# Where three small pieces of work stand in the order of an attention kernel: a reciprocal, two gate activations and a projection

## The chip, the cores and the metric

The kernel runs on one core of a Trainium2 chip. Its time is the device time of one execution in microseconds. Before the change three executions took 1186.85, 1190.78 and 1191.3 us, the median being 1190.78 us. The profiled execution is a fourth one, and took 1187.66 us.

## The reference

Four sequences of 1024 tokens with 128 channels pass through one block: causal attention with 16 heads of 64 and a bias by distance, a residual and a layer norm, then an RWKV channel mix, a residual and a second layer norm.

```python
q, k, v = einsum('bsx,xMnd->Mbnsd', x, qkv)
a = softmax(einsum('bnsd,bntd->bnst', q, k) * 64**-0.5 + bias)      # bias: cumsum by distance, -30000 above the diagonal
x = layernorm(x + einsum('bnsd,ndx->bsx', einsum('bnst,bntd->bnsd', a, v), out_w))
x_prev = x shifted by one token
r = sigmoid((mu_r * x + (1 - mu_r) * x_prev) @ W_r.T)
k = square(relu((mu_k * x + (1 - mu_k) * x_prev) @ W_k.T))
x = layernorm(x + r * (k @ W_v.T))
```

## The kernel before

Two heads make a pair; 4 sequences times 8 pairs are 32 steps (`PAIR_STEPS`). Every engine has its own program, written out by hand as a loop over the steps and, in each step, over 16 slots (`NROWS`). A slot stands for one score row: one head and one tile of 128 queries, 128 to 1024 keys wide. Slots 0 to 3 are head 0, tiles 0 to 3; 4 to 7 head 1, tiles 0 to 3; 8 to 11 head 0, tiles 4 to 7; 12 to 15 head 1, tiles 4 to 7. No planner moves anything: an engine does its instructions in the order of its own loop, and semaphores hold it until what it needs is there.

A row goes through the engines like this. TensorE (PE) computes its scores four slots ahead (line 954). VectorE (DVE) adds the bias from PSUM and takes the row minimum in one instruction (line 643; the scores are negated, so the minimum is the maximum). ScalarE (ACT) takes the exponential with its sum (line 486), also four slots ahead. In the row's own slot PE transposes its blocks of 128x128 (line 968) into one of two PSUM banks, `ps_t0` and `ps_t1`, which alternate: bank use k may start once use k-2 has been copied out. A row of up to 4 blocks is one bank use, a longer row two. `EVACUATOR` says who copies use k out: DVE (line 667) or ACT (line 504). Uses 8 and 9 belong to slot 8, 10 and 11 to slot 9, 12 and 13 to slot 10, 14 and 15 to slot 11, 16 and 17 to slot 12, 18 and 19 to slot 13, 20 and 21 to slot 14, 22 and 23 to slot 15. Uses 8, 10, 11, 12, 14, 16 and 20 are DVE's, uses 9, 13, 15, 17, 18, 19, 21, 22 and 23 are ACT's. In slot 14 the inverses of the sums (DVE, line 653, issued in slot 13) are transposed as well (line 973).

Between these rows stands other work. The next step's q, k and v are projected in six chunks at `PROJ_SLOTS`, all into the one bank `ps_m`: four chunks of two matmuls of 512 columns (line 929), and two chunks of four blocks for v, in slots 10 and 14 (line 934). ACT copies a v chunk out (line 476) at the beginning of the same slot. The probabilities are multiplied with v in slots 2 and 5 for the upper half of the step before, and in slot 11 for the lower half (line 992).

From step 9 on (`TILE_LAG`), each step also takes one tile of 128 tokens of an earlier sequence through the rest of the block (`tile_step`); step 31 and the code behind the loop do what is left. 23 of the 32 steps have such a tile, and 22 of these (9 to 30) project for a next step too. Slot 0: the output projection (PE line 1006), which needs `mix_tile`, a 512 KB load that SyncE issues at line 353 behind the eight transfers of the k stacks. Slots 1, 2 and 4: first layer norm and token shift. Slot 9: receptance and key projections (PE lines 1011 and 1012), the exponential of the gate and the relu of the key on ACT (lines 521 and 522, semaphore `s_sig`), then 1 + exp and the square on DVE. Slot 11: the gate's reciprocal on DVE (line 713). Slot 12: the v projection (PE line 1016), product with the gate, residual and statistics on DVE. Slot 15: second layer norm (ACT lines 514 and 517, DVE line 724). These tile matmuls also use `ps_m`: a projection chunk or tile matmul starts only when ACT or DVE has read the one before out of it (`wait_chunk`, `wait_tile`). So the v chunk in slot 10 waits for `s_sig`, that is for ACT's relu.

Within a slot the orders that the change touches are these. ACT: copy of a projection chunk, the tile's activations, copies of its bank uses, exponential of the row four slots ahead. DVE: bias and minimum of the row four slots ahead, inversion of sums, `lo` part of a projection chunk, copies of its bank uses, multiplication of a finished mix, the tile's step; in slot 8 alone the copies come first. PE: scores of the row four slots ahead, projection chunk, tile matmul, mix, transposes of the own row.

Of the kernel before, what the change touches and what calls it, by code (L numbers as in the profile page):

```python
# [13 lines left out]
PAIR_STEPS = BATCH * PAIRS  # L14
# [26 lines left out]
def score_at(r):  # L41


    if r < NROWS // 2:
        return BANK * (r % 4)
    width = P * (ROWS[r][1] + 1)
    return SEQ * (r % 2) + ((SEQ - width) // 2 if width - BANK < SHORTEST else 0)
# [22 lines left out]

EVACUATED = [evacuated(engine, NBANKS) for engine in range(2)]

PROJ_SLOTS = (2, 3, 5, 7, 10, 14)
NPROJ = len(PROJ_SLOTS)


OUT_PROJ, LN1_RSTD, LN1 = 0, 1, 2
# [3 lines left out]
RK_PROJ, GATE = 9, 11  # L81
# [11 lines left out]
def build(nc, x, qkv, out_w, rpe, w_r, w_k, w_v, mu_r, mu_k, out):  # L93
# [14 lines left out]
    with ExitStack() as ctx:  # L108
# [6 lines left out]
        def sem(name):  # L115
            return ctx.enter_context(nc.semaphore(name))
# [86 lines left out]
        s_v = sem("v_ready")  # L203
# [58 lines left out]
        def rows_ahead(n, more, slot):  # L262

            if slot + LEAD < NROWS:
                return [(n, slot + LEAD)]
            return [(n + 1, slot + LEAD - NROWS)] if more else []
# [176 lines left out]
        def _(act):  # L443
# [15 lines left out]
            def project(m, c):  # L459

                if c == 0 and m > 0:
                    if m == 1:
                        act.wait_ge(s_first, 96)
                    for h in range(2):
                        act.wait_ge(s_stack[h], 96 * m)
                act.wait_ge(s_proj, NPROJ * m + c + 1)
                if c < 4:
                    which, at = chunk_of(m, c)
                    dst, scale = ((q_hi, SCALE), (k_hi, 1.0))[which]
                    half = slice(512 * at, 512 * at + 512)  # L470
                    nc.scalar.activation(dst[:, half], proj_bank(m, c), ACT.Copy, scale=scale).then_inc(s_hi, 1)  # L471
                else:
                    half = slice(4 * (c - 4), 4 * (c - 4) + 4)
                    if c == 4 and m >= 2:
                        act.wait_ge(s_pv, 2 * m)
                    nc.scalar.activation(v_pair[m % 2][:, half, :],  # L476
                                         proj_bank(m, c).rearrange("p (t d) -> p t d", d=P), ACT.Copy).then_inc(s_v, 1)

            def exps(n, r):

                width = P * (ROWS[r][1] + 1)
                act.wait_ge(s_biased, NROWS * n + r + 3)
                if n > 0 and r % (2 * GROUP) == 0:
                    act.wait_ge(s_inv, 2 * n - 1 + r // (2 * GROUP))
                row = prob[:, r % PSLOTS, 0:width]
                nc.scalar.activation(row, row, ACT.Exp, bias=low[:, r:r + 1], scale=-1.0,  # L486
                                     accum_out=total[:, r:r + 1]).then_inc(s_exp, 1)

            def evacuate(n, k, tile_too):
                r, b0, nb = BANKS[k]  # L490
                h, i = ROWS[r]
                g = i // GROUP
                act.wait_ge(s_pv, 2 * n + g + 1)
                if n == 0 and r == 3 * GROUP:
                    act.wait_ge(s_xt_dram, 16 * (BATCH - 1))
                act.wait_ge(s_tr, NBANKS * (n + 1) + k + 1)
                if k == X1_BANK and tile_too:
                    at = 1 + (n - TILE_LAG) % TILES * P
                    nc.scalar.activation(x1_t[:, at:at + P], ps_t[k % 2][:, P:2 * P], ACT.Copy).then_inc(s_x1t, 1)
                if k == INV_BANK[1]:  # L500
                    if n > 0:
                        act.wait_ge(s_inv_d[1], 16 * n)
                    nc.scalar.activation(inv_t[1][:, :], ps_t[k % 2][0:2 * GROUP, 3 * P:], ACT.Copy).then_inc(s_inv_t[1], 1)
                nc.scalar.activation(pt[h][g][:, b0:b0 + nb, P * (i % GROUP):P * (i % GROUP) + P],  # L504
                                     ps_t[k % 2][:, 0:nb * P].rearrange("p (b s) -> p b s", s=P),
                                     ACT.Copy).then_inc(s_ev[1], 1)
# [33 lines left out]
            def step(n, prev, tile_too, more):  # L540
                for slot in range(NROWS):
                    if more and slot in PROJ_SLOTS:
                        project(n + 1, PROJ_SLOTS.index(slot))
                    if tile_too:
                        tile_step(n, slot)
                    for k in range(NBANKS):
                        if BANKS[k][0] == slot and EVACUATOR[k] == "1":
                            evacuate(n, k, tile_too)
                    for row in rows_ahead(n, more, slot):
                        exps(*row)  # L550

            drive(step)

            def ln_rstd(which, w):
# [48 lines left out]
        def _(dve):  # L603
# [29 lines left out]
            def bias(n, r):  # L633

                h, i = ROWS[r]
                width = P * (i + 1)
                if i % GROUP == 0:
                    dve.wait_ge(s_table[n % 2][h], 16 * (n // 2) + 16)

                before = (r - PSLOTS) % NROWS  # L640
                dve.wait_ge(s_tr, NBANKS * (n if before > r else n + 1) + sum(b[0] <= before for b in BANKS))
                dve.wait_ge(s_score, NROWS * n + r + 1)
                nc.vector.tensor_tensor_reduce(prob[:, r % PSLOTS, 0:width],  # L643
                                               ps_rows[:, score_at(r):score_at(r) + width],
                                               table[n % 2][:, h, 0:width][:, ::-1], 1.0, 3.0e38, ALU.add, ALU.min,
                                               low[:, r:r + 1]).then_inc(s_biased, 1)
# [96 lines left out]
            def step(n, prev, tile_too, more):  # L743
                for slot in range(NROWS):
                    if slot == LATE_SLOT:
                        empty_banks(n, slot)
                    for row in rows_ahead(n, more, slot):
                        bias(*row)
                    if slot in INV_READY:
                        invert(n, INV_READY.index(slot))  # L750
                    if more and slot in PROJ_SLOTS[:4]:
                        project(n + 1, PROJ_SLOTS.index(slot))
                    if slot != LATE_SLOT:
                        empty_banks(n, slot)
                    if prev and slot == MIX_FAR[1] + 1:
                        store_mix(n - 1, 1)
                    if slot == MIX_NEAR + 1:
                        store_mix(n, 0)
                    if tile_too:
                        tile_step(n, slot)  # L760

            drive(step)
# [103 lines left out]
        def _(pe):  # L866
# [28 lines left out]
            def wait_chunk(m, c):  # L895

                if 0 <= c < 4:
                    pe.wait_ge(s_lo, 4 * m + c + 1)
                else:
                    pe.wait_ge(s_v, 2 * m + (c - 3 if c > 0 else 0))  # L900
# [10 lines left out]
            def project(m, c, tile_too):  # L911
# [13 lines left out]
                if tile_too:  # L925
                    wait_tile(m - 1 - TILE_LAG, sum(at < PROJ_SLOTS[c] for at in TILE_MATMULS))
                if c < 4:
# [69 lines left out]
            def tile_step(n, slot, more=False):  # L997
                e = n - TILE_LAG
                if more and slot in TILE_MATMULS:
                    wait_chunk(n + 1, sum(at <= slot for at in PROJ_SLOTS) - 1)  # L1000
                if slot in TILE_MATMULS:
                    wait_tile(e, TILE_MATMULS.index(slot))
                if slot == OUT_PROJ:
                    pe.wait_ge(s_mixt, 16 * e + 16)
                    for p in range(PAIRS):
                        ins = nc.tensor.matmul(ps_m[:, 0:C], mix_tile[:, p, :], wo[:, p, :],  # L1006
                                               start=(p == 0), stop=(p == PAIRS - 1))
                    ins.then_inc(s_e1, 1)
                if slot == RK_PROJ:
                    pe.wait_ge(s_chain, CH * (e + 1) + 6)  # L1010
                    nc.tensor.matmul(ps_m[:, 0:P], xr_t[:, :], w_t[:, 0, :], start=True, stop=True)
                    nc.tensor.matmul(ps_m[:, P:2 * P], w_t[:, 1, :], xk_t[:, :], start=True, stop=True)\
                        .then_inc(s_e6, 1)
                if slot == V_PROJ:
                    pe.wait_ge(s_chain, CH * (e + 1) + 7)
                    nc.tensor.matmul(ps_m[:, 0:C], k_act[:, :], w_t[:, 2, :], start=True, stop=True).then_inc(s_e8, 1)
# [126 lines left out]
```

## Time and profile before

| | |
|---|---|
| median of three executions | 1190.78 us (1186.85 to 1191.3) |
| profiled execution, its own time | 1187.66 us |
| its span | 1185.9 us |
| granted TensorE clock, mean | 0.992 |
| PE busy | 1115.7 us (94%) |
| DVE busy | 811.5 us (68%) |
| ACT busy | 727.4 us (61%) |
| PE's longest wait in total | 23.1 us in 42 waits, for DVE's copies of `ps_t` |

The profile is one execution. The span is what the records cover; 1.76 us of the execution's own time lie around it. From one step's v chunk to the next step's it is 35.40 us in steps with a tile, and 33.24 us in steps without. Busy time of PE counts matmuls with modelled, overlapping ends, so the start of one group to the start of the next tells more than the durations.

### The profile page before, as it was taken

To read this page: it belongs to the slowest core of one execution; us is meant where nothing else is said; L and a number is where in the kernel's file an instruction comes from. 1 tells how busy PE (TensorE), PEld (TensorE's weight loads), DVE (VectorE), ACT (ScalarE), POOL (GpSimd) and SP (SyncE) were. 2 spreads that over 40 slices of the span, in tenths; PEclk is the share of its full clock that TensorE was granted. 3 is DMA by queue.
4 is the path that set the end of the run, shared out by engine and by line. 5 is a ranking of instruction groups with operands and counts; after the bars stand their busy time and mean duration, and the time that the engine had idled before them with its cause. 6 is when DMAs were issued, how large, how long until landed. Compare 5 with 4: busy or idle time off the path is not lost.

```text
span 1185.9 us, 21563 instructions
## 1 busy us (share of the span) xinstructions
PE 1115.7 (94%) x6973; PEld 783.3 (66%) x6973; DVE 811.5 (68%) x2121; ACT 727.4 (61%) x1857; POOL 6.4 (1%) x15
## 2 busy tenths in 40 slices
PE   5999999989999999999999999999999999999994
PEld 3666666666666667666667666676666667767673
DVE  2666666666667677767677767677767677777756
ACT  3666666666666666666566656566656666656632
POOL 1000000000000000000000000000000000000000
PEclk9999999999999999999999999999999999999997
DMA  8865556565655666656657655657665657665610
GB/s 213 215 150 140 136 137 150 136 177 145 154 150 142 158 153 173 160 143 161 157 150 180 159 145 141 151 150 202 155 149 139 150 153 180 155 154 136 223 55 20
DMA packets 113005, 180.71 MB, mean 152 GB/s; under 512 B 13152, under 2 KB 69360, under 8 KB 112896
## 3 DMA queue, kind: packets, MB, share of 16 engines
q1 hardware_dynamic: 110736, 178.42, 59.5%
q8 instruction: 58, 0.95, 0.3%
q10 hardware_dynamic: 2160, 0.92, 0.3%
q14 instruction: 51, 0.42, 0.1%
HBM read 58.41 MB, written 20.22 MB: 66 GB/s over the span
## 4 chain that ended last, share of the span: by engine, by line
PE 82%; DVE 8%; ACT 5%; issue 4%; DMA 1%; DVEq 0%; SPq 0%; POOL 0%; ACTq 0%
PE ps_o L992 22%; PE ps_t L968 21%; PE ps_rows L954 18%; PE ps_m L929 9%; PE ps_m L934 5%; PE ps_m L1006 4%; DVE pt L667 3%; DVE prob L643 3%; ACT prob L486 3%; PE ps_rows L1062 1%; DMA prob<-in_L_attn_x 1%; ACT pt L504 1%; PE ps_t L973 1%; DVE mix_sb L674 1%; ACT xk_t L522 1%
## 5 line engine op out<-in xcount | busy, mean ns | idle before, releaser
L486 ACT ACTIVATE prob<-prob,low 128x128 f32<-128x128 f32 (+7 forms) x512 | 394.6, 772 | 129.4 <-DVE low L643 125.1
L643 DVE CUSTOM_DVE_ANT_0 prob<-ps_rows,table 128x128 f32<-128x128 f32 (+7 forms) x512 | 378.8, 748 | 56.2 <-PE ps_rows L954 55.4
L954 PE MATMUL ps_rows<-stacks 128*128 128x512 f32 (+3 forms) x1536 | 401.9, 372 | 6.3 <-issue 4.4
L968 PE MATMUL ps_t<-ident,prob 128*128 128x128 f32 x2304 | 347.2, 277 | 30.7 <-DVE pt L667 23.1
L968 PEld LDWEIGHTS ps_t<-ident,prob 128*128 128x128 f32 x2304 | 261.0, 140 | 134.7 <-issue 96.2
L667 DVE COPY pt<-ps_t 128x512 f32<-128x512 f32 (+3 forms) x352 | 200.4, 577 | 178.8 <-PE ps_t L968 176.9
L992 PE MATMUL ps_o<-pt,v_pair 128*64 128x512 f32 (+3 forms) x1536 | 268.6, 492 | 0.0
L954 PEld LDWEIGHTS ps_rows<-stacks 128*128 128x128 f32 x1536 | 246.0, 190 | 27.1 <-issue 4.6
L504 ACT ACTIVATE pt<-ps_t 128x512 f32<-128x512 f32 (+3 forms) x416 | 187.2, 466 | 114.6 <-PE ps_t L968 114.3
L992 PEld LDWEIGHTS ps_o<-pt,v_pair 128*64 128x64 f32 x1536 | 101.8, 136 | 181.7 <-issue 172.3
L929 PE MATMUL ps_m<-x_cur,w_cur 128*128 128x512 f32 x250 | 130.8, 605 | 2.5 <-issue 1.6
L471 ACT ACTIVATE q_hi<-ps_m 128x512 fp32r<-128x512 f32 x63 | 37.4, 593 | 122.1 <-PE ps_m L929 121.8
L486 ACT ACTIVATION_READ_ACCUMULATOR prob<-prob,low 128x1 f32 x512 | 97.8, 191 | 0.0
L629 DVE SCALAR_TENSOR_TENSOR q_lo<-ps_m,q_hi 128x512 fp32r<-128x512 f32 x63 | 43.6, 692 | 50.8 <-ACT q_hi L471 50.8
L934 PE MATMUL ps_m<-w_cur,x_cur 128*128 128x128 f32 x504 | 68.0, 278 | 6.4 <-ACT xk_t L522 6.4
L934 PEld LDWEIGHTS ps_m<-w_cur,x_cur 128*128 128x128 f32 x504 | 63.6, 191 | 13.0 <-issue 12.9
L929 PEld LDWEIGHTS ps_m<-x_cur,w_cur 128*128 128x128 f32 x250 | 43.4, 191 | 14.5 <-issue 8.0
L1006 PE MATMUL ps_m<-wo,mix_tile 128*128 128x128 f32 x384 | 47.0, 275 | 0.1
L629 DVE SCALAR_TENSOR_TENSOR k_lo<-ps_m,k_hi 128x512 fp32r<-128x512 f32 x62 | 42.6, 687 | 4.8 <-ACT k_hi L471 4.7
L1006 PEld LDWEIGHTS ps_m<-wo,mix_tile 128*128 128x128 f32 x384 | 44.9, 192 | 0.5 <-issue 0.4
L476 ACT ACTIVATE v_pair<-ps_m 128x512 f32<-128x512 f32 x63 | 37.3, 592 | 12.7 <-PE ps_m L934 11.2
L674 DVE TENSOR_TENSOR mix_sb<-ps_o,inv_all 128x512 f32<-128x512 f32 x64 | 43.6, 681 | 2.0 <-PE ps_o L992 2.0
(114 smaller groups left out, 475.2 us busy)
## 6 DMA issues: line engine op xcount, KB each, us to landing
stacks<-k_hi SPq DMA_DIRECT2D x126, 256.0 KB, 4.5
stacks<-k_lo SPq DMA_DIRECT2D x126, 256.0 KB, 4.9
inv_all<-inverse_sums SPq DMA_DIRECT2D x128, 128.0 KB, 3.3
stacks<-q_hi SPq DMA_DIRECT2D x63, 256.0 KB, 3.8
stacks<-q_lo SPq DMA_DIRECT2D x63, 256.0 KB, 4.3
mix_transposed<-mix_sb SPq DMA_DIRECT2D x62, 256.0 KB, 2.3
table<-bias_by_distance SPq DMA_DIRECT2D x64, 192.0 KB, 3.6
mix_tile<-mix_transposed SPq DMA_DIRECT2D x24, 512.0 KB, 5.3
```

Source lines behind the costliest of these rows:

```text
L486: nc.scalar.activation(row, row, ACT.Exp, bias=low[:, r:r + 1], scale=-1.0, accum_out=total[:, r:r + 1]).then_inc(s_exp, 1)
L504: nc.scalar.activation(pt[h][g][:, b0:b0 + nb, P * (i % GROUP):P * (i % GROUP) + P], ps_t[k % 2][:, 0:nb * P].rearrange("p (b s) -> p b s" ...
L629: nc.vector.scalar_tensor_tensor(out=lo[:, half], in0=proj_bank(m, c), scalar=scale, in1=hi[:, half].bitcast(F32), op0=ALU.mult, op1=ALU.s ...
L643: nc.vector.tensor_tensor_reduce(prob[:, r % PSLOTS, 0:width], ps_rows[:, score_at(r):score_at(r) + width], table[n % 2][:, h, 0:width][:, ...
L667: nc.vector.tensor_copy(pt[h][g][:, b0:b0 + nb, P * (i % GROUP):P * (i % GROUP) + P], ps_t[k % 2][:, 0:nb * P].rearrange("p (b s) -> p b s ...
L674: nc.vector.tensor_tensor(mix_sb[g][:, :], ps_o[:, :], inv_all[g][:, :], ALU.mult).then_inc(s_o, 1)
L929: ins = nc.tensor.matmul(proj_bank(m, c), w_cur[m % 2][:, which, :], x_cur[:, 512 * at:512 * at + 512], start=True, stop=True)
L934: ins = nc.tensor.matmul(proj_bank(m, c)[:, P * t:P * t + P], x_cur[:, at:at + P], w_cur[m % 2][:, 2, :], start=True, stop=True)
L954: ins = nc.tensor.matmul(ps_rows[:, at + c0:at + c1], q_st(h, n)[:, P * i:P * i + P], k_st(h, n, low_part)[:, c0:c1], start=(low_part == 0 ...
L968: ins = nc.tensor.transpose(ps_t[k % 2][:, P * b:P * b + P], prob[:, r % PSLOTS, at:at + P], ident[:, :])
L992: ins = nc.tensor.matmul(ps_o[D * h:D * h + D, c0:], v_pair[n % 2][:, j, D * h:D * h + D], pt[h][g][:, j, c0:], start=(j == 0), stop=(j == ...
L1006: ins = nc.tensor.matmul(ps_m[:, 0:C], mix_tile[:, p, :], wo[:, p, :], start=(p == 0), stop=(p == PAIRS - 1))
```

## The change

Three groups of instructions change place; none is added or removed, but for one semaphore wait on PE.

1. The second v chunk goes from slot 14 to slot 15, on PE and on ACT (`PROJ_SLOTS`). With it, `wait_chunk` for the chunk before is evaluated for the new slot, and in the last step PE waits ahead of the output projection for the last v copy.
2. On ACT the tile's two activations of slot 9 (`RK_PROJ`) are issued in slot 8, behind ACT's copy of bank use 9 and ahead of the exponential of row 12.
3. On DVE the gate's reciprocal in slot 11 is issued directly behind the bias and minimum of row 15, ahead of the copy of bank use 14.

```diff
--- before.py
+++ after.py
@@ -70,7 +70,7 @@
 
 EVACUATED = [evacuated(engine, NBANKS) for engine in range(2)]
 
-PROJ_SLOTS = (2, 3, 5, 7, 10, 14)
+PROJ_SLOTS = (2, 3, 5, 7, 10, 15)
 NPROJ = len(PROJ_SLOTS)
 
 
@@ -541,11 +541,13 @@
                 for slot in range(NROWS):
                     if more and slot in PROJ_SLOTS:
                         project(n + 1, PROJ_SLOTS.index(slot))
-                    if tile_too:
+                    if tile_too and slot != RK_PROJ:
                         tile_step(n, slot)
                     for k in range(NBANKS):
                         if BANKS[k][0] == slot and EVACUATOR[k] == "1":
                             evacuate(n, k, tile_too)
+                    if tile_too and slot + 1 == RK_PROJ:
+                        tile_step(n, RK_PROJ)
                     for row in rows_ahead(n, more, slot):
                         exps(*row)
 
@@ -746,6 +748,8 @@
                         empty_banks(n, slot)
                     for row in rows_ahead(n, more, slot):
                         bias(*row)
+                    if tile_too and slot == GATE:
+                        tile_step(n, slot)
                     if slot in INV_READY:
                         invert(n, INV_READY.index(slot))
                     if more and slot in PROJ_SLOTS[:4]:
@@ -756,7 +760,7 @@
                         store_mix(n - 1, 1)
                     if slot == MIX_NEAR + 1:
                         store_mix(n, 0)
-                    if tile_too:
+                    if tile_too and slot != GATE:
                         tile_step(n, slot)
 
             drive(step)
@@ -998,6 +1002,8 @@
                 e = n - TILE_LAG
                 if more and slot in TILE_MATMULS:
                     wait_chunk(n + 1, sum(at <= slot for at in PROJ_SLOTS) - 1)
+                if n == PAIR_STEPS - 1 and slot == OUT_PROJ:
+                    pe.wait_ge(s_v, 2 * PAIR_STEPS)
                 if slot in TILE_MATMULS:
                     wait_tile(e, TILE_MATMULS.index(slot))
                 if slot == OUT_PROJ:
```

## Rows read from the trace of the kernel before

**Rows 1.** The page: the chain that ended last, shares by engine.

```profile
PE 82%; DVE 8%; ACT 5%; issue 4%; DMA 1%; DVEq 0%; SPq 0%; POOL 0%; ACTq 0%
```

**Rows 2.** Waits of PE, whole span: total us, times, longest.

```profile
PE ps_t L968 <- DVE pt L667: 23.1, 42, 0.8
PE ps_m L934 <- ACT xk_t L522: 6.4, 22, 0.3
```

**Rows 3.** Timeline, a step with a tile, slots 8 to 10: start, duration, what.

```profile
631.90 0.39 PE L1012 MATMUL ps_m<-xk_t,w_t 128*128 128x128 f32 x2
632.79 0.83 ACT L486 ACTIVATE prob<-prob,low 128x640 f32<-128x640 f32 x1 [0.54 <-DVE low L643]
632.81 1.09 PE L954 MATMUL ps_rows<-stacks 128*128 128x512 f32 x4
633.62 0.26 ACT L521 ACTIVATE shift<-ps_m 128x128 f32<-128x128 f32 x1
633.78 0.27 ACT L522 ACTIVATE xk_t<-ps_m 128x128 f32<-128x128 f32 x1
634.19 1.13 PE L934 MATMUL ps_m<-w_cur,x_cur 128*128 128x128 f32 x8 [0.29 <-ACT xk_t L522]
635.16 0.93 PE L968 MATMUL ps_t<-ident,prob 128*128 128x128 f32 x7
```

**Rows 4.** Timeline, a step without a tile, slots 10 to 13.

```profile
212.67 1.08 PE L954 MATMUL ps_rows<-stacks 128*128 128x512 f32 x4
213.59 1.05 PE L934 MATMUL ps_m<-w_cur,x_cur 128*128 128x128 f32 x8
214.48 0.93 PE L968 MATMUL ps_t<-ident,prob 128*128 128x128 f32 x7
220.17 0.74 PE L968 MATMUL ps_t<-ident,prob 128*128 128x128 f32 x5 [0.27 <-DVE pt L667]
221.74 0.85 PE L968 MATMUL ps_t<-ident,prob 128*128 128x128 f32 x6 [0.60 <-DVE pt L667]
```

**Rows 5.** Timeline, the step with a tile again, slots 11 to 13.

```profile
640.01 0.69 DVE L667 COPY pt<-ps_t 128x512 f32<-128x512 f32 x1 [1.62 <-PE ps_t L968]
640.62 0.94 DVE L713 RECIPROCAL shift<-xr_t 128x128 f32<-128x128 f32 x1
640.85 0.74 PE L968 MATMUL ps_t<-ident,prob 128*128 128x128 f32 x5
642.46 0.84 PE L968 MATMUL ps_t<-ident,prob 128*128 128x128 f32 x6 [0.64 <-DVE pt L667]
```

**Rows 6.** Timeline, the same step, slots 13 to 15, and slot 0 of the next.

```profile
643.19 0.87 ACT L504 ACTIVATE pt<-ps_t 128x512 f32<-128x512 f32 x2 [0.48 <-PE ps_t L968]
643.50 1.05 PE L934 MATMUL ps_m<-w_cur,x_cur 128*128 128x128 f32 x8
644.38 0.93 PE L968 MATMUL ps_t<-ident,prob 128*128 128x128 f32 x7
645.18 0.72 PE L954 MATMUL ps_rows<-stacks 128*128 128x512 f32 x2
645.93 1.06 PE L968 MATMUL ps_t<-ident,prob 128*128 128x128 f32 x8
647.07 1.17 PE L1006 MATMUL ps_m<-wo,mix_tile 128*128 128x128 f32 x9
```

**Rows 7.** Timeline, slot 3 of that step: scores 512 wide, then a projection chunk.

```profile
619.38 0.71 PE L954 MATMUL ps_rows<-stacks 128*128 128x512 f32 x2
619.93 1.02 PE L929 MATMUL ps_m<-x_cur,w_cur 128*128 128x512 f32 x2
```

**Rows 8.** ACT's 512-wide copies out of `ps_t`, steps with a tile, by form: busy, mean ns.

```profile
L504 ACT ACTIVATE pt<-ps_t 128x512 f32<-128x512 f32 x138 | 79.3, 592 | 77.5 <-PE ps_t L968 77.4
```

**Rows 9.** The load of `mix_tile`: when issued in that step, then all 24 to landing.

```profile
640.93 1.19 SPq L353 DMA_DIRECT2D mix_tile<-mix_transposed  x1
DMA to landing us min/median/max: 4.3/5.3/5.9
```

## The prediction, made before the changed kernel was run

> **What bounds the kernel now.** The page's chain that ended last comes first: 82% of it is PE, 8% DVE and 5% ACT [rows 1]. So an instruction moved on DVE or ACT is worth only what it takes from a wait of PE, and PE's own waits come next. The longest by far is for DVE's copies of `ps_t`, 23.1 us in 42 waits; then 6.4 us in 22 waits for ACT's relu at line 522, once in each of the 22 steps that have a tile and project for a next step [rows 2]. Each part of the change stands beside one of these, and the timeline of one step with a tile and of one without shows where. I measure from the start of one PE group to the start of the next, because the ends overlap.
>
> **Part 2: ACT's gate activations ahead of row 12's exponential.** Before, ACT waits 0.54 us for DVE's minimum of row 12, starts that exponential at 632.79, and only then does the gate's exponential (633.62) and the relu (633.78 to 634.05). PE's v chunk of slot 10 starts 0.14 us behind the relu, at 634.19 [rows 3]. That 0.14 us is my latency from ACT to PE throughout. After the change ACT can start as soon as the matmuls of line 1012 are done, 631.90 + 0.39 = 632.29; its waits behind PE are some 0.04 to 0.09 us, so the gate starts at about 632.35, the relu 0.16 us later (633.78 - 633.62), and it ends at 632.78. Row 12's exponential could start at 632.79 before; now it starts then or up to 0.1 us later, and its reader, the transposes of slot 12, is at 640.85 [rows 5]. PE no longer waits: relu plus 0.14 us is 632.92. What is late next is PE itself, behind the scores of row 14. How soon it goes on is seen in the step without a tile, where the same groups stand without that wait: scores to transposes 214.48 - 212.67 = 1.81 us [rows 4], against 635.16 - 632.81 = 2.35 us with a tile [rows 3]. The gain is 0.54 us, more than the 0.29 us that the wait's own row names, since that row starts counting at the modelled end of the last matmul. By that smaller figure it would be 0.29 us; these are my two bounds, and I take 0.54, because it is a difference of like groups. 22 x 0.54 = 11.9 us (by the lower bound 6.4 us).
>
> The new wait on ACT, for line 1012, is in no row. What queues behind it is row 12's exponential, then row 13's and the copies of uses 13 and on. From below it costs nothing (the wait ends at 632.3 inside the idle 0.54 us); from above the two activations push the exponential by 0.32 us, their two spacings of 0.16 us. Neither end reaches PE, so I take nothing.
>
> **Part 3: DVE's reciprocal ahead of the copy of use 14.** It takes 0.94 us at 640.62, right behind that copy. DVE had been idle for 1.62 us before the copy began at 640.01 [rows 5], so in its new place the reciprocal lies in that idle time, with some 0.7 us to spare. Nobody queued behind it is late: the copy comes at the same moment. What goes away is the reciprocal ahead of the copy of use 16, which PE waits for before slot 13. But that wait is mostly a round trip: PE transposes four blocks, DVE copies, PE goes on into the same bank. Without any reciprocal, in the step without a tile, PE still needs 221.74 - 220.17 = 1.57 us [rows 4], against 642.46 - 640.85 = 1.61 us with it [rows 5]. So the gain is 0.04 us, 22 x 0.04 = 0.9 us; bounds: 0, and 0.64 us if the whole wait went. The row that shows the same pair of groups decides.
>
> **Part 1: the second v chunk from slot 14 to slot 15.** It adds no work, but it fills a gap now. Transposes of row 13 start at 642.46; ACT starts to copy their first bank (use 18) at 643.19 [rows 6], which takes 0.59 us [rows 8], so PE may refill it at 643.19 + 0.59 + 0.14 = 643.92, that is 1.46 us behind. Before, PE did six blocks, row 2's scores and the v chunk meanwhile and came to row 14 at 644.38, without a wait. Without the chunk it is free at 643.50, and waits 0.42 us. From there (643.92): transposes of row 14 and of the sums 645.18 - 644.38 = 0.80 us, row 3's scores up to a following projection 619.93 - 619.38 = 0.55 us [rows 7], the v chunk 644.38 - 643.50 = 0.88 us [rows 6]. Row 15's transposes start at 643.92 + 2.23 = 646.15, not 645.93 [rows 6]. The gap that the chunk could fill in slot 15 is smaller: row 3's scores would let PE on at 645.18 + 0.55 = 645.73, so PE waited 0.20 us for DVE's copy of use 20. One wait of 0.20 is filled, one of 0.42 opened: 0.22 us lost. This happens in all 31 steps that project: 31 x 0.22 = 6.8 us. Bounds: 0.20 us gained (no new wait) and 0.42 us lost (none filled).
>
> [...]
>
> The moved copy of v on ACT: PE's chunk would run from 645.27 for 1.05 us, the copy (0.6 us) ends at about 646.95 and PE may read on at 647.1; the output projection, which now waits for it, comes at 646.15 + (647.07 - 645.93) = 647.3 [rows 6]. 0.2 us in hand: nothing is lost. SP issues nothing earlier or later in its own order; the table, weight and stack loads keep their places.
>
> **A transfer that may come late.** `mix_tile` is issued at 640.93, behind the k stacks, whose time hangs on slot 7, ahead of all this. Landing takes 4.3 to 5.9 us, median 5.3 [rows 9]: 646.2, and 646.8 at worst. A step with a tile reaches the output projection 0.54 + 0.04 - 0.22 = 0.36 us earlier, at 646.71. The median landing is still in time, the latest few would hold PE by 0.1 to 0.2 us. I put 0.5 us on this (bounds 0, and 2.5 us were all as late as the worst). [...]
>
> **Sum.** -11.9 - 0.9 + 6.8 + 0.5 = -5.5 us, from the profiled execution's own 1187.66 us (span 1185.9 and 1.8 around it) to 1182.2. That execution lies 3.1 us under the median of 1190.78; the mean of all four executions is 1189.1. I set the sum against that mean: 1183.6 us. That is 0.46% less. A difference of 0.5% (5.9 us) is about the least that a measurement of this kernel can tell from no change.
>
> **Rivals.**
> (a) The filler's move is free: PE doesn't wait for use 18 in slot 14, or the slot 15 wait was larger than 0.20 us. For it: PE's start times are modelled. Against: the round trip of 1.46 us is the same as in the pairs of [rows 4, 5]. Time 1189.1 - 12.3 = 1176.8.
> (b) The wait of slot 10 gives only its 0.29 us, the rest being there anyhow: -6.4 - 0.9 + 6.8 = -0.5 us, 1188.6. For it: the wait's own row [rows 2]. Against: the like groups [rows 4].
> (c) ACT becomes what PE waits for in slot 0: the v copy of slot 15 goes behind row 2's exponential, and if ACT comes to it later than the 0.2 us in hand, the output projection is late. If one more 0.6 us instruction of ACT lies ahead, 22 x 0.6 = 13.2 us come on top: -5.5 + 13.2 = +7.7, 1196.8, slower. For it: ACT has the sums' transpose, use 21 and that exponential in a row there. Against: ACT idles 0.48 us just before [rows 6].
> (d) The change doesn't do what it says: ACT's wait for line 1012 ends so late that row 13's exponential is late too and PE gets nothing of part 2: -0.9 + 6.8 = +5.9, 1195.0.
>
> **Numbers.** The forecast 0.60, (a) 0.15, (b) 0.13, (c) 0.08, (d) 0.04. Predicted 1183.6; range 1177.5 to 1190, which takes in (b), nearly (a), and the spread of executions. The forecast's own 0.60 lies close to the threshold and splits 0.29 faster, 0.31 same. Faster by over 0.5%: 0.29 + 0.15 = 0.44. Same: 0.31 + 0.13 + 0.01 = 0.45. Slower: 0.11.
>
> **What would show it.** ACT line 522 ahead of row 12's exponential and PE's waits for it gone, step period with a tile 0.36 us shorter and without 0.22 us longer; the reciprocal in DVE's idle time behind row 15's minimum; slot 12 to slot 13 at 1.57 us; a new wait of PE on ACT line 504 in slot 14, about 0.4 us in 31 steps, and no wait on line 667 in slot 15. Wrong would be a step without a tile that doesn't get longer, or a wait ahead of line 1006.

## The result and the profile after

The changed kernel takes 1184.29 us (median of 8 executions, 1181.35 to 1187.95), the kernel before 1189.85 us (8 executions, 1185.18 to 1191.3). The ratio is 0.9959, with a 95% interval of 0.9939 to 0.9978: 4.9 us faster, or 0.4%. The forecast was 0.46% faster at 1183.6 us. The profiled execution took 1184.52 us, its span is 1182.8 us, against 1187.66 and 1185.9 us before.

The page's chain that ended last looks almost as in [rows 1], but transfers have gone from 1% to 3% of it.

```profile
PE 81%; DVE 6%; ACT 4%; issue 4%; DMA 3%; SPq 1%; DVEq 0%; POOL 0%; ACTq 0%
```

PE's waits over the whole span (us in total, times, longest) answer to [rows 2]. The wait for ACT's relu is gone. The wait for ACT's copies of `ps_t` has grown from 2.7 us in 11 waits to 11.3 us in 42, and some waits for transfers have come.

```profile
PE ps_t L972 <- DVE pt L669: 19.8, 38, 0.8
PE ps_t L972 <- ACT pt L504: 11.3, 42, 0.6
PE ps_rows L958 <- DMA stacks<-k_lo: 1.8, 5, 0.5
PE ps_m L1012 <- DVE o_tile L726: 0.5, 1, 0.5
```

The timeline of one step with a tile, slots 8 to 10, answers to [rows 3] (start, duration, what):

```profile
632.66 0.39 PE L1018 MATMUL ps_m<-xk_t,w_t 128*128 128x128 f32 x2
633.09 0.28 ACT L521 ACTIVATE shift<-ps_m 128x128 f32<-128x128 f32 x1
633.26 0.27 ACT L522 ACTIVATE xk_t<-ps_m 128x128 f32<-128x128 f32 x1
633.56 0.83 ACT L486 ACTIVATE prob<-prob,low 128x640 f32<-128x640 f32 x1
633.58 1.09 PE L958 MATMUL ps_rows<-stacks 128*128 128x512 f32 x4
634.51 1.05 PE L938 MATMUL ps_m<-w_cur,x_cur 128*128 128x128 f32 x8
635.40 0.93 PE L972 MATMUL ps_t<-ident,prob 128*128 128x128 f32 x7
```

The gate starts 0.04 us behind the end of line 1018 (632.66 + 0.39 = 633.05). The relu is over at 633.53, and row 12's exponential starts at 633.56 without an idle time in front of it: the two activations fit exactly into what was ACT's 0.54 us of waiting. PE goes from the scores to the transposes in 635.40 - 633.58 = 1.82 us (2.35 before; 1.81 was forecast).

The same step, slots 11 to 15, answers to [rows 5, 6]:

```profile
637.42 1.23 DVE L645 CUSTOM_DVE_ANT_0 prob<-ps_rows,table 128x1024 f32<-128x1024 f32 x1
638.57 0.95 DVE L715 RECIPROCAL shift<-xr_t 128x128 f32<-128x128 f32 x1
640.27 0.69 DVE L669 COPY pt<-ps_t 128x512 f32<-128x512 f32 x1 [0.75 <-PE ps_t L972]
641.11 0.74 PE L972 MATMUL ps_t<-ident,prob 128*128 128x128 f32 x5
642.68 0.84 PE L972 MATMUL ps_t<-ident,prob 128*128 128x128 f32 x6 [0.60 <-DVE pt L669]
643.40 0.87 ACT L504 ACTIVATE pt<-ps_t 128x512 f32<-128x512 f32 x2 [0.43 <-PE ps_t L972]
644.14 0.95 PE L972 MATMUL ps_t<-ident,prob 128*128 128x128 f32 x7 [0.27 <-ACT pt L504]
644.96 0.71 PE L958 MATMUL ps_rows<-stacks 128*128 128x512 f32 x2
645.51 1.05 PE L938 MATMUL ps_m<-w_cur,x_cur 128*128 128x128 f32 x8
646.40 1.04 PE L972 MATMUL ps_t<-ident,prob 128*128 128x128 f32 x8
646.60 0.60 ACT L476 ACTIVATE v_pair<-ps_m 128x512 f32<-128x512 f32 x1
647.51 1.95 PE L1012 MATMUL ps_m<-wo,mix_tile 128*128 128x128 f32 x16
```

The reciprocal lies in DVE's idle time, of which 0.75 us is left (1.62 us before). Slot 12 to slot 13 is 642.68 - 641.11 = 1.57 us, slot 13 to slot 14 is 1.46 us, and slot 13 to slot 15 is 646.40 - 642.68 = 3.72 us (3.47 before; 3.69 was forecast). ACT's v copy ends at 647.20, 0.31 us ahead of the output projection.

A step is measured below from the start of its first v chunk (slot 10, which no part of the change moves) to that of the next. There are 30 such intervals, 8 without a tile and 22 that run from or into a step with one. The value that the shortest of each kind share within 0.03 us is called the floor. In the kernel before, 18 of the 22 steps with a tile keep to it, in the changed kernel 13, and in the fastest kernels without earlier transfers only 3 to 6. The sum of what the single steps lie above the floor is called the excess. It is read from one execution of each kernel.

| | ratio to before | with a tile | without | excess, 30 steps | of it in the 22 steps with a tile |
|---|---|---|---|---|---|
| before | 1 | 35.40 | 33.24 | 3.5 | 0.8 |
| changed kernel | 0.9959 | 35.06 | 33.48 | 5.3 | 3.6 |

### The profile page after: what moved, and what is told of

It reads as the page before. It is cut to its first block, busy times and chain, and to the rows that moved or that the text cites. A ratio compares the mean times of both kernels' runs of the same rounds, so it can differ in the third digit from the quotient of the medians.

```text
span 1182.8 us, 21563 instructions
## 1 busy us (share of the span) xinstructions
PE 1111.7 (94%) x6973; PEld 785.7 (66%) x6973; DVE 814.4 (69%) x2121; ACT 733.3 (62%) x1857; POOL 6.4 (1%) x15
## 2 busy tenths in 40 slices
DMA packets 113005, 180.71 MB, mean 153 GB/s; under 512 B 13152, under 2 KB 69360, under 8 KB 112896
## 3 DMA queue, kind: packets, MB, share of 16 engines
q1 hardware_dynamic: 110736, 178.42, 59.8%
## 4 chain that ended last, share of the span: by engine, by line
PE 81%; DVE 6%; ACT 4%; issue 4%; DMA 3%; SPq 1%; DVEq 0%; POOL 0%; ACTq 0%
PE ps_o L996 22%; PE ps_t L972 21%; PE ps_rows L958 19%; PE ps_m L933 8%; PE ps_m L938 4%; PE ps_m L1012 4%; ACT pt L504 2%; DVE pt L669 2%; DMA stacks<-k_lo 2%; DVE prob L645 1%; DMA prob<-in_L_attn_x 1%; PE ps_rows L1068 1%; SPq L288 1%; ACT prob L486 1%; DVE mix_sb L676 1%
```

## The experiments

**The three parts, each alone.** Theory: the terms of the prediction, ACT -0.54 us and reciprocal -0.04 us in each of 22 steps, slot +0.22 us in each of 31. The rivals are those of the prediction. First the ACT part:

```diff
-                    if tile_too:
+                    if tile_too and slot != RK_PROJ:
                         tile_step(n, slot)
...
+                    if tile_too and slot + 1 == RK_PROJ:
+                        tile_step(n, RK_PROJ)
                     for row in rows_ahead(n, more, slot):
                         exps(*row)
```

> The kernel before with the ACT part alone: the tile's two gate activations ahead of row 12's exponential. Theory: steps with a tile go from 35.40 to 34.86 us (0.54 us less) where no transfer is late, steps without stay at 33.24; the wait of PE for line 522 is gone. 22 x 0.54 = 11.9 us, less 2 to 4 us of waits for the k stacks, which are not issued any earlier: 8 to 10 us faster, ratio 0.992 to 0.993. Rival (b) of the prediction: 0.29 us a step, 6.4 us before the waits for transfers, ratio 0.997 or more.

Measured: ratio 0.9948 (0.9932 to 0.9964), 6.2 us faster. The floor is 34.86 us with a tile, which is the 0.54 us to the hundredth, and 33.24 without. But the excess is 10.8 us, 6.4 of it in the steps with a tile. The mechanism and the size per step are the theory's and not rival (b)'s. What arrives in the median is half of the 11.9 us, less than the 8 to 10 us that were expected: the interval of the ratio lies above 0.993. PE's waits in this kernel, from 60 to 1125 us, name transfers where the kernel before had hardly any:

```profile
PE ps_m L1008 <- DMA mix_tile<-mix_transposed: 1.3, 2, 0.8
PE ps_m L1008 <- DVE o_tile L726: 0.7, 2, 0.4
PE ps_rows L956 <- DMA stacks<-k_lo: 0.6, 3, 0.3
```

Then the slot alone:

```diff
-PROJ_SLOTS = (2, 3, 5, 7, 10, 14)
+PROJ_SLOTS = (2, 3, 5, 7, 10, 15)
...
+                if n == PAIR_STEPS - 1 and slot == OUT_PROJ:
+                    pe.wait_ge(s_v, 2 * PAIR_STEPS)
```

> The kernel before with the second v chunk alone moved to slot 15. Theory: each of 31 steps 0.22 us longer (35.62 with a tile, 33.46 to 33.48 without), a wait of PE for ACT's copy of use 18 of 0.4 us in slot 14, 6.8 us slower in all, ratio 1.006. Rival (a): the move is free, ratio 1.000, no new wait of more than 0.2 us.

Measured: 1.0044 (1.003 to 1.0058), 5.2 us slower; the 1.006 that was expected lies just outside. The floors are 35.63 and 33.48 us: 0.23 and 0.24 us more. This part by itself makes the kernel slower, and rival (a) is out. Its excess is only 3.1 us. PE's new wait, whole span:

```profile
PE ps_t L968 <- DVE pt L667: 23.2, 42, 0.8
PE ps_t L968 <- ACT pt L504: 11.3, 42, 0.6
PE ps_m L934 <- ACT xk_t L522: 6.5, 22, 0.3
```

The rows carry a lesson. The wait in slot 14 is 0.42 us by the arithmetic, but the figure in brackets in its timeline row says 0.27, and the 31 waits that this list has more than the one before the change come to 8.6 us, 0.28 us each. The wait is counted from the modelled end of the last matmul, and that is 0.15 us behind the moment at which PE could have gone on (in slot 10 it was 0.54 - 0.29 = 0.25 us).

The reciprocal alone:

```diff
+                    if tile_too and slot == GATE:
+                        tile_step(n, slot)
                     if slot in INV_READY:
                         invert(n, INV_READY.index(slot))
...
-                    if tile_too:
+                    if tile_too and slot != GATE:
                         tile_step(n, slot)
```

> The kernel before with the reciprocal alone moved ahead of the copy of use 14. Theory: slot 12 to slot 13 goes from 1.61 to 1.57 us, nothing else; steps with a tile 35.36 us, 0.9 us in all, not to be told from no change (ratio 0.999). Rival: the whole wait of 0.64 us on DVE's copy goes, 14 us, ratio 0.988.

Measured: 0.9994 (0.9982 to 1.0006), the floor 35.35 us, 0.05 us less. As expected it can't be told from no change, and the 0.6 us of waiting for DVE stays.

**Without the slot move.** The two useful parts together, the v chunk back in slot 14 (the first and the third of the diffs above):

> The changed kernel without its slot move: ACT part and reciprocal, v chunk in slot 14. Theory: steps with a tile 34.82 us where no transfer is late, without 33.24; 12.8 us before late transfers, of which more than in the changed kernel are late (PE is 0.24 us earlier in each step), so 9 to 11 us faster than before, ratio 0.991 to 0.992, and some 4 to 5 us faster than the changed kernel. Rival: the parts don't add, because the slot move made room for the ACT part; then it is no faster than the changed kernel, ratio 0.996.

Measured: 0.994 (0.9917 to 0.9963), floors 34.83 and 33.24 us. In the floor the parts add within 0.02 us: 0.57 us against 0.54 + 0.05. But the ratio missed what was expected (0.991 to 0.992), and the excess has grown to 14.0 us. The profiled execution was the slowest of the six (1186.75 us, the median is 1181.46), so this figure is a high one. Against the changed kernel the ratio is only 0.0019 better, less than the intervals can tell. PE's waits over the whole span, and one of them in the timeline:

```profile
PE ps_m L1010 <- DMA mix_tile<-mix_transposed: 4.7, 5, 1.4
PE ps_rows L958 <- DMA stacks<-k_lo: 1.5, 3, 1.0
```

```profile
470.69 0.48 PE L958 MATMUL ps_rows<-stacks 128*128 128x256 f32 x2
472.54 2.02 PE L1010 MATMUL ps_m<-wo,mix_tile 128*128 128x128 f32 x16 [1.37 <-DMA mix_tile<-mix_transposed]
```

Of the waits for the stacks 1.0 us is one at 54.67 us, in the first step, which has its like in the kernel before (0.53 us).

The excess over 30 steps rises with how much earlier PE is in the floor: 3.1 us in the slower kernel, 3.5 before, 4.9 with the reciprocal alone, 5.3 changed, 10.8 with the ACT part, 14.0 with both. But two things are mixed in it. In the 22 steps with a tile it is 1.7, 0.8, 1.2, 3.6, 6.4 and 9.5 us, in the same order. In the steps without a tile, 3.3 to 3.5 us in three of the six profiles (reciprocal alone, ACT part alone, both) lie in one step, where PE waits before the first chunk of a new sequence; 1.2 to 1.9 us lie there in the others. In these three the granted TensorE clock fell to 0.50 for 3.4 us after that wait, and with both parts the chunk took 1.91 us; in the kernel before it stayed at 1.00 after a longer wait, and the chunk took 1.10 us. The two rows, with both parts and before:

```profile
264.04 1.91 PE L933 MATMUL ps_m<-x_cur,w_cur 128*128 128x512 f32 x2 [1.40 <-issue]
262.80 1.10 PE L929 MATMUL ps_m<-x_cur,w_cur 128*128 128x512 f32 x2 [1.64 <-issue]
```

Why the clock fell in some executions and not in others is open. It is no property of a kernel: in the second profile of the ACT part alone, further down, it stayed at 1.00 there. In the steps with a tile the granted clock was 1.00 in all these profiles. What is left there fits a faster PE that meets transfers which don't come any sooner. That they are the cause was tested next.

**A second look at the ACT part.**

> A second profile of the kernel with the ACT part alone: does the time above 34.86 us a step (6.4 us over 22 steps in the first profile) fall on the same steps? Theory: it comes from transfers whose time to landing varies, so the sum stays between 3 and 10 us, on partly other steps. Rival: a fixed cost of certain steps, the same steps with the same amounts.

One execution, 1178.2 us, on another chip than the first six (1181.76 to 1183.91 us), while the kernel before took the same on both (1188.67 and 1188.62 us): excess 4.9 us in the 22 steps with a tile (6.4 in the first profile), 7.1 us in all 30 (10.8). Seven of its steps lie more than 0.25 us above the floor, nine in the first profile, and six of them are the same. But the amounts differ: a step that lay 0.79 us above in the first lies 0.02 us above in the second. Both readings hold in part: certain steps are more exposed than others, and how late they are varies from execution to execution.

**The transfers issued sooner.** SP sends the first 512 columns of head 0's keys, all that rows 0 to 3 of the next step read, as soon as slot 5's chunk is there; their second half, needed four slots into the next step, goes last, behind the load of `mix_tile`. A semaphore of its own holds row 8's scores for it. The bytes are the same, in four transfers more per step.

```diff
                 store_inverse(n, 0)
+                if more:
+                    sp.wait_ge(s_lo, 4 * n + 7)
+                    stack_k(n + 1, 0, s_stack[0], first)
...
-                    for h in range(2):
-                        stack_k(n + 1, h, s_stack[h])
+                    stack_k(n + 1, 1, s_stack[1])
                 if n + 1 >= TILE_LAG:
                     tile_loads(n + 1 - TILE_LAG)
+                if more:
+                    stack_k(n + 1, 0, s_far, second)
```

On the kernel with ACT part and reciprocal:

> ACT part and reciprocal without the slot move, and the transfers that came late issued sooner: the first 512 columns of head 0's keys go out as soon as slot 5's chunk is there, the mix tile's load goes ahead of their second half. Theory (late transfers ate part of the gain): the steps keep to 34.83 us with a tile and 33.24 without, with less than 3 us of excess in all 30 steps against 14 us without this; 12 to 15 us faster than before, ratio 0.988 to 0.990. Rival: the excess is not from these two transfers but from more DMA work in less time; then the excess stays at 9 us or more and the ratio at 0.994.

Measured: 0.988 (0.9867 to 0.9893), median 1174.78 us. The excess falls from 14.0 to 3.8 us (from 9.5 to 2.1 us in the steps with a tile, of which 1.8 is one wait for another load, of `x_cur`). That is a little more than the 3 us expected and far below the rival's 9. The floors are still 34.83 and 33.24 us. The load of `mix_tile` takes even longer to land than before (median 6.3 us against 5.3, [rows 9]) and PE never waits for it. PE's waits from 60 to 1125 us name neither transfer:

```profile
PE ps_t L981 <- DVE pt L676: 21.6, 41, 0.8
PE ps_t L981 <- ACT prob L493: 2.6, 8, 0.3
PE ps_t L981 <- ACT pt L511: 2.1, 10, 0.6
PE ps_m L940 <- DMA x_cur<-x_transposed: 1.8, 1, 1.8
```

The same on the changed kernel, and on the kernel before as the control:

> The changed kernel with the same earlier transfers. Theory: steps at 35.06 us with a tile and 33.48 without, no excess from transfers; 22 x 0.34 - 9 x 0.24 = 5.3 us and the excess of 3.6 us: 7 to 9 us faster than before, ratio 0.993 to 0.994. Rival: as the changed kernel, 0.996.

Measured: 0.9923 (0.991 to 0.9937), 9.2 us faster, floors 35.06 and 33.48, excess 1.3 us, of which 0.15 us in the steps with a tile (3.6 without the earlier transfers).

> The kernel before with the same earlier transfers, as the control. Theory: PE meets hardly any late transfer in the kernel before (0.8 us of excess in steps with a tile), so 0 to 2 us faster, ratio 0.998 to 1.000, steps at 35.40 and 33.24 us. Rival: the transfers' order is worth several us by itself, ratio 0.995 or less.

Measured: 0.998 (0.9967 to 0.9993), floors 35.40 and 33.24, excess 1.9 us, 0.3 us of it in the steps with a tile. The order of the transfers is worth 0.2% where PE is slow, 0.36% on the changed kernel (0.9959 to 0.9923), and 0.6% where PE is fastest (0.994 to 0.988). The last two compare ratios taken on different chips, each against the kernel before on its own, and each is uncertain by some 0.25%; the second profile above suggests, by one execution, that a kernel can lie 0.4% apart between two chips. So their sizes are rough. The cause doesn't hang on them: on one chip the ACT part alone has 4.9 us of excess in its steps with a tile, and the last kernel below, which is faster still in the floor but has the earlier transfers, has 0.2 us. That excludes the rival that more DMA work in less time slowed everything, since as many bytes move in less time there (180.73 MB in 1170.2 us, against 180.71 MB in 1181.2 us with the ACT part alone). The larger part of the gain is no gain of its own but the recovery of one that had been given back.

**A gap that is worth filling.** If PE's waits between bank uses are round trips, the v chunk belongs where the largest of them lies: ahead of slot 13's transposes (0.60 us in [rows 4]). Steps with a tile can't have it there, since the tile's v projection holds `ps_m`; steps without can.

```diff
+EARLY_SLOTS = PROJ_SLOTS[:5] + (13,)
...
+                slots = PROJ_SLOTS if tile_too else EARLY_SLOTS
                 for slot in range(NROWS):
-                    if more and slot in PROJ_SLOTS:
-                        project(n + 1, PROJ_SLOTS.index(slot))
+                    if more and slot in slots:
+                        project(n + 1, slots.index(slot))
```

> The kernel before with the second v chunk in slot 13 instead of 14 in the steps without a tile alone. Theory of the gaps between bank uses: the chunk (0.88 us) fills the wait of 0.60 us before slot 13's transposes and makes them 0.12 us later; the gap before slot 14 opens again but with 0.46 us less from slot 13 to 14 (1.46 us round trip against 1.92 us). Steps without a tile go from 33.24 to 32.90 us, steps with one stay at 35.40: 9 x 0.34 = 3 us, ratio 0.997 to 0.998. Rival: slots 13 to 15 are bound by the sum of PE's work, and where the chunk stands makes no difference: 33.24 us.

Measured: 0.9971 (0.996 to 0.9982). The floor of steps without a tile is 32.90 to 32.93 us, that of steps with one 35.40. The timeline of a step without a tile, slots 12 to 14:

```profile
220.15 0.74 PE L970 MATMUL ps_t<-ident,prob 128*128 128x128 f32 x5 [0.27 <-DVE pt L669]
220.96 1.06 PE L936 MATMUL ps_m<-w_cur,x_cur 128*128 128x128 f32 x8
221.85 0.82 PE L970 MATMUL ps_t<-ident,prob 128*128 128x128 f32 x6
222.55 0.87 ACT L505 ACTIVATE pt<-ps_t 128x512 f32<-128x512 f32 x2
223.29 0.96 PE L970 MATMUL ps_t<-ident,prob 128*128 128x128 f32 x7 [0.26 <-ACT pt L505]
```

Slot 13 comes 1.70 us behind slot 12 (1.57 before), slot 14 then 1.44 us behind slot 13 (1.92 before). The 0.60 us wait is filled, and the 0.4 us wait (0.26 in its row) opens, as in the changed kernel. The same chunk gains 0.33 us in slot 13 and loses 0.24 us in slot 15, both against slot 14; the rival that only PE's sum of work counts is out.

All of it together:

> The ACT part, the reciprocal and the earlier transfers, with the second v chunk in slot 13 in the steps without a tile and in slot 14 in those with one. If the parts add: 34.83 us with a tile, 32.90 without, 3 us less than the same kernel with the chunk in slot 14 throughout, ratio to the kernel before 0.985 to 0.986.

Measured: 0.9861 (0.9844 to 0.9877), median 1171.81 us, floors 34.83 and 32.91, excess 1.9 us, 0.2 us of it in the steps with a tile. This version is 1.4% faster than the kernel before and, by the ratios, 1.0% faster than the changed one; the version with the chunk in slot 14 throughout is 1.2% and 0.8% faster. Between these two the difference is 0.0019 where 0.0025 was expected, less than their intervals can tell.

## Why the prediction was right

- **ACT part.** Forecast -0.54 us a step, measured 35.40 - 34.86 = 0.54. The choice between the two bounds was the point: the wait's own row said 0.29 us, the comparison of like groups in steps with and without the wait 0.54, and the second was right. That ACT's new wait costs nothing is shown too: the relu ends 0.03 us before row 12's exponential starts, though that is no margin to build on.
- **Reciprocal.** Forecast -0.04, measured -0.05 alone and -0.03 beside the ACT part. The wait that it seemed to cause is a round trip of PE, DVE and PE (1.57 us from slot 12 to slot 13), and stays.
- **Slot.** Forecast +0.22, measured +0.23 and +0.24. It opens one gap (0.42 us by the arithmetic, 0.27 us in its row) and fills a smaller one (0.20 us by the forecast's arithmetic). With the chunk in slot 15 the two banks alone don't cover ACT's copy of use 18: PE comes to row 14 1.46 us behind row 13.
- **Late transfers.** This is the mis-sized term. Forecast 0.5 us, all on `mix_tile`, with waits of 0.1 to 0.2 us. In the steps with a tile, the only ones to which the forecast applied it, the excess grew by 3.6 - 0.8 = 2.8 us between the two profiles. In the 8 steps without a tile it fell by 0.9 us, for which the prediction had no term, and the sum is 1.8 us. The experiments with earlier transfers put the value of the whole excess at 0.36% on the changed kernel against 0.2% before; the difference of 0.16%, or 1.9 us, is smaller than its uncertainty. Six waits from 60 us on come from transfers by name or by what follows. Four are for the stack of head 0's keys at slot 12, 1.3 us in all, and behind three of them row 13's transposes wait for an exponential that is late, 0.6 us each. This stack the prediction passed over: it looked at whether SP's order changed, and not at whether PE came sooner. One of 0.3 us is for `x_cur`. The sixth was the load foreseen, under another name. Ahead of the output projection at 858.76 the timeline names a DVE instruction, but PE waits there for nothing that this instruction writes. The load for this tile was issued at 852.43 and took 6.2 us to land, which is 858.6 and longer than any in [rows 9]. A wait ahead of the output projection was on the prediction's own list of signs of being wrong; this one came, once in the profile. The two rows, the second a view of that load alone:

```profile
858.76 2.02 PE L1012 MATMUL ps_m<-wo,mix_tile 128*128 128x128 f32 x16 [0.46 <-DVE o_tile L726]
```

```profile
mix_tile<-mix_transposed SPq DMA_DIRECT2D x1, 512.0 KB, 6.2
```

- **Sum.** Forecast -5.5 us and 1183.6 us, measured 1184.29. With the measured floors the sum is -22 x 0.34 + 9 x 0.24 = -5.3 us, and the 1.8 us by which the excess grew give -3.5; the two profiled executions differ by 3.1 us, the medians by 5.6, the ratio says 4.9 with 2.6 to 7.3 around it. So the sum is right within what can be measured. That the medians differ by almost exactly the forecast's 5.5 us, although its last term was 1.3 to 2.3 us too small, is luck.
- **Rival (c)** did not happen: the v copy ended 0.31 us ahead of the output projection, where the forecast had 647.3 - 646.95 = 0.35 us; less the 0.14 us from ACT to PE, 0.17 us was in hand (0.2 forecast). Rival (d) is excluded by the ACT part alone.

What stays open is how the excess divides between the two transfers, since both were issued sooner at once, and how large it is on average, since it was read from one or two executions of each kernel.

## What to carry to other kernels

Price a wait by the distance between the same two groups with and without it, not by the idle time in its row, which starts at a modelled end (0.54 us against 0.29 us here). Work that stands between two uses of a PSUM bank pair is a filler: put it in the largest gap, and count the gap it leaves (here the same chunk gained 0.33 us a step in slot 13 and lost 0.24 us in slot 15). When the bounding engine gets faster, list every transfer that it meets and how late each may land; here part of what the change gained was given back there (up to half in the ACT part alone), and most of it returned when the half of head 0's keys that is read first was sent first and the other half last. Before adding up small delays over a whole kernel, look at the granted clock and at single steps: one step with a granted clock of 0.50 held 3.3 to 3.5 us.

## What the runs showed of the hardware

With this kernel's two banks of four 128x128 transposes each, the refill of a PSUM bank came 1.46 us behind the first transposes when ACT copied 512 columns out (642.68 to 644.14), and 1.57 us when DVE did (641.11 to 642.68). Of these the copies are 0.59 and 0.69 us, and from their end to PE it is 0.14 to 0.15 us. In the experiments PE's wait in such a round trip went away only where other matmuls stood in it, as in slot 13, where the v chunk of 0.88 us took the place of 0.60 us of waiting.

The transfers of the k stacks in the changed kernel landed after 2.4 to 6.8 us (median 4.8), with their queue taking 59.8% of the 16 DMA engines' time. That is wide against steps that otherwise repeat to 0.03 us.

The granted TensorE clock fell from 1.00 to 0.50 for 3.4 us behind a wait of PE of 1.4 to 1.6 us in three profiles, and stayed at 1.00 behind a wait of 1.64 us at the same place in the kernel before.
